# Corner and MLP sums on GpSimd, a norm pass in place, VectorE's and TensorE's order in the slots, image 1's convolutions in two parts, and a reordered ramp

## The reference

```
x_ln = layernorm(x) * g + b
q    = x_ln @ wq + bq                                # 1024 rows
o    = gelu(depthwise_conv7x7(q, stride 2) + dw_b)   # 16 x 16 positions
off  = tanh(o @ pw_w)                                # 2 numbers per position
samp = bilinear samples of x at (reference point + off)   # 256 rows, 4 corners each
qh, kh, vh = (q @ mq, (samp@wv+bv) @ mk, (samp@wv+bv) @ mv)   # 8 heads of 32
att  = softmax(qh kh^T) vh                           # 1024 x 256 scores per head
z    = att @ mo + mo_b + x
y    = gelu(layernorm(z) @ mlp + mlp_b) + z
theta, phi, g = y @ w_theta, maxpool(y @ w_phi), maxpool(y @ w_g)   # biases added
out  = y + sigma * (softmax(theta phi^T) g @ w_o + b_o)
```

## Time and profile before

| | |
|---|---|
| median of 3 runs | 595.2 us (594.95 to 597.31) |
| the profiled execution, its own time | 598.47 us |
| its span, first to last instruction | 596.5 us |
| mean granted clock of TensorE | 0.90 |
| TensorE busy | 476.4 us (80% of the span) |
| VectorE busy | 311.1 us (52%) |
| ScalarE busy | 198.5 us (33%) |
| GpSimd busy | 86.5 us (15%) |

### The profile page before, as it was taken

How to read it: one execution, slowest core, us unless ns; L and a number is a source line. 1 busy time by engine, 2 the same in 40 slices (tenths; PEclk the granted TensorE clock), 3 DMA queues, 4 the chain that set the end, 5 groups by cost and what they waited for, 6 DMA issues and landing times.

```text
span 596.5 us, 9174 instructions
## 1 busy us (share of the span) xinstructions
PE 476.4 (80%) x3711; PEld 332.3 (56%) x3711; DVE 311.1 (52%) x664; ACT 198.5 (33%) x313; POOL 86.5 (15%) x120
## 2 busy tenths in 40 slices
PE   0699477887779998976899998967986896898746
PEld 0556254564447765644578665644864574666425
DVE  5635553155387443575795326665643556444242
ACT  1011100253334323651435206623263272335420
POOL 2401101052101000610001003501001041000000
PEclk9999678877798998896999997978988998899878
DMA  8596269724803970274016901363019000000001
GB/s 230 114 170 91 74 80 131 170 73 63 99 0 46 118 188 1 72 96 61 6 73 93 181 6 30 77 73 55 37 48 166 1 2 1 2 37 36 0 1 71
DMA packets 28695, 42.89 MB, mean 72 GB/s; under 512 B 5819, under 2 KB 17902, under 8 KB 28654
## 3 DMA queue, kind: packets, MB, share of 16 engines
q1 hardware_dynamic: 20894, 35.23, 34.9%
q0 software_dynamic: 3584, 4.50, 2.8%
q10 hardware_dynamic: 4176, 2.58, 1.6%
HBM read 16.16 MB, written 4.19 MB: 34 GB/s over the span
## 4 chain that ended last, share of the span: by engine, by line
PE 57%; DVE 19%; ACT 8%; DMA 8%; issue 5%; POOL 1%; SPq 1%; DVEq 0%; ACTq 0%; POOLq 0%
PE ps_d L642 8%; PE ps_d L632 5%; DMA q_st<-mx_t 5%; PE ps_v L722 5%; PE ps_d L836 4%; PE ps_d L737 4%; PE ps_t L709 4%; PE ps_v L726 4%; PE ps_s L690 4%; PE ps_d L760 4%; DVE mx L1378 4%; PE ps_d L670 2%; PE ps_d L779 2%; PE ps_d L661 2%; DMA corners<-in_L_conv_mlp_b_dram 2%
## 5 line engine op out<-in xcount | busy, mean ns | idle before, releaser
L1054 ACT ACTIVATE prob<-ps_t 128x1024 f32<-128x1024 f32 x64 | 65.4, 1021 | 111.6 <-PE ps_t L709 110.7
L1378 DVE TENSOR_REDUCE mx<-ps_s 128x4 f32<-128x1024 f32 x64 | 78.2, 1222 | 27.9 <-PE ps_s L690 26.7
L1650 POOL DMA_DIRECT2D q_st<-mx_t x64 | 34.0, 532 | 362.6 <-ACT mx_t L1046 347.9
L690 PE MATMUL ps_s<-k_st,q_st 96*128 96x256 f32 x256 | 51.3, 325 | 10.8 <-DVE mx L1378 5.6
L642 PE MATMUL ps_d<-cstack,conv_w 128*32 128x256 f32 x1024 | 59.0, 388 | 0.4 <-DMA cstack<-qpad 0.4
L709 PE MATMUL ps_t<-q_st,k_st 98*128 98x256 f32 x256 | 45.9, 306 | 9.9 <-DMA q_st<-mx_t 8.4
L690 PEld LDWEIGHTS ps_s<-k_st,q_st 96*128 96x128 f32 x256 | 37.8, 202 | 22.1 <-DVE mx L1378 8.8
L642 PEld LDWEIGHTS ps_d<-cstack,conv_w 128*32 128x32 f32 x1024 | 34.4, 111 | 25.4 <-issue 6.0
L632 PE MATMUL ps_d<-wq,xln 128*128 128x256 f32 x128 | 33.8, 425 | 15.0 <-DVE xln L1270 15.0
L709 PEld LDWEIGHTS ps_t<-q_st,k_st 98*128 98x128 f32 x256 | 38.6, 208 | 11.7 <-DMA q_st<-mx_t 9.0
L722 PE MATMUL ps_v<-prob,vh 128*32 128x256 f32 x512 | 42.0, 455 | 0.0
(11 more groups left out here) (161 smaller groups left out, 723.8 us busy)
## 6 DMA issues: line engine op xcount, KB each, us to landing
q_st<-q_parts SPq DMA_DIRECT2D x48, 256.0 KB, 8.5
cstack<-qpad SPq DMA_DIRECT2D x24, 180.5 KB, 5.3
xa<-in_x_dram SPq DMA_DIRECT2D x8, 512.0 KB, 12.6
z_all<-in_x_dram SPq DMA_DIRECT2D x4, 1024.0 KB, 14.2
out_dram<-z_all SPq DMA_DIRECT2D x8, 512.0 KB, 2.6
k_st<-cstack SPq DMA_DIRECT2D x12, 256.0 KB, 6.2
cstack<-att SPq DMA_DIRECT2D x8, 180.5 KB, 7.0
q_st<-mx_t POOLq DMA_DIRECT2D x64, 4.0 KB, 2.5
```

The source lines that it names most:

```text
L690: ins = pe.matmul(ps_s[:, h, :], q_st[0:96, hg * HQ + h, c0 + half * P:c0 + (half + 1) * P], k_st[0:96, b % 2, h, hg, :], start=True, stop ...
L1054: drain(act.activation(prob[:, u % 2, 2 * pr:2 * pr + 2].rearrange("p h m s -> p (h m) s"), ps_t[:], ACT.Exp), t_ring, "t", b, u, pr)
L1378: drain(dve.tensor_reduce(mx[:, u % 2, half, :], ps_s[:], AX.X, ALU.max), s_ring, "s", b, u, half)
L1650: pool.dma_start(q_st[96 + part:97 + part, hg * HQ:(hg + 1) * HQ, c0:c0 + S_].bitcast(F32), mx_t[32 * part:32 * part + HQ, u % 2, :].bitca ...
```

## The change

Seven things are changed together.

1. **Corner sums on GpSimd.** For images 1 to 3 `sampled` is moved from VectorE (slot 6, or 5 for image 1) to GpSimd in slot 5, as eight products and six sums in place of two products and six fused steps. The keys of image 1 move from slot 5 to 6. Image 0's corner sums stay on VectorE, in the ramp.
2. **MLP sums on GpSimd.** `outputs` of images 0 to 2 goes to GpSimd, slots 1 and 4. `bias_rows` moves from slot 4 to 6. The tail's stay on VectorE.
3. **The norm's first pass in place**, `xa` into `xa`, as `row_scale`; the second pass is `row_shift`. The statistics move from slot 7 to slot 4 (for image 2 to slots 3 and 4), `row_scale` to slot 5 (and 6), `row_shift` stays in slot 7, whole for image 2; for image 3 a half of it is left for the next slot 0, as before for both. Image 1's normed rows lie in `z[1]`, and a part of image 0's queries in `z[0]`, which are loaded later.
4. **VectorE's order.** The maxima of scores come ahead of `residual_norm` in slot 0; `query_lo(n, 1)` comes ahead of the maxima in slot 7; the second block's maxima follow at once.
5. **TensorE's order.** The convolution's second half (`conv1`) stands behind the scores and shifted scores of slot 3; image 1's two convolutions are each cut in 6 and 10 of 16 steps, around the second half of the scores; `queries(n, 1)` leads slot 7; `q_image(n, 0)` comes before `turn_rows` in slot 0; in slot 7 a projection stands before each shifted product of the second block; `vh` of image 0 is in slot 0.
6. **The ramp.** The norm's two rows g and b are loaded first, on ScalarE's queue; the copies of folded weights are on ScalarE; the fold for the queries stands before `q_image(0, 0)`; `queries(0, 1)` goes around the offsets; `q_image(1, 0)` stands before the keys; the convolution's weights are built in two halves; image 0's planes are stacked from two queues.
7. **Positions** take 5 dependent steps in place of 7, with constants prepared on the host.

The core of the diff:

```diff
-FRONT_SLOTS_OF_1 = {"conv0": 1, "conv1": 2, "off": 3, "qh0": 4, "kh": 5, "qh1": 7}
+FRONT_SLOTS_OF_1 = {"conv0": 1, "conv1": 2, "off": 3, "qh0": 4, "kh": 6, "qh1": 7}
+FIRST_STEPS, LAST_STEPS = range(6), range(6, TAPS * TAPS)
...
@@ GpSimd @@
+            def outputs(b, cb):
+                for jp in range(2):
+                    k = dense.use("mlp", b, cb, jp)
+                    part = z[b % 2][:, cb, 2 * jp:2 * jp + 2, :]
+                    pool.wait_ge(k.drained, k.done)
+                    pool.tensor_tensor(part, part, norm_tile(b, cb)[:, 2 * jp:2 * jp + 2, :], ALU.add).then_inc(y_done.sem, 1)
+
+            def sampled(b):
+
+                pool.wait_ge(ramp_step.sem, ramp_step.at(b, 6))
+                for st in range(2):
+                    pool.wait_ge(corners_in[st].sem, corners_in[st].at(b, 2))
+                    if st == 0:
+
+                        k = dense.use("vh", b - 1)
+                        pool.wait_ge(k.filled, k.full)
+                    for n in range(4):
+                        below, right = divmod(n, 2)
+                        corner = corners[:, st, below, right * C:(right + 1) * C]
+                        weight = corner_w[:, below, right, st:st + 1]
+                        pool.tensor_scalar(corner if n else samp[:, st, :], corner, weight, None, ALU.mult
+                                           ).then_inc(weighted.sem if n else samp_step.sem, 1)
+                    for n in range(1, 4):
+                        below, right = divmod(n, 2)
+                        pool.wait_ge(weighted.sem, weighted.at(b - 1, 3 * st + n))
+                        pool.wait_ge(samp_step.sem, samp_step.at(b, 4 * st + n))
+                        pool.tensor_tensor(samp[:, st, :], samp[:, st, :], corners[:, st, below, right * C:(right + 1) * C],
+                                           ALU.add).then_inc(samp_step.sem, 1)
...
                 if in_front(b, s, "off"):
                     gather(n)
+                if s == 1 and 0 <= m < B:
+                    outputs(m, 0)
+                if s == 4 and 0 <= m < B:
+                    outputs(m, 1)
+                if s == 5 and n < B:
+                    sampled(n)
                 if s == 7 and 0 <= m < B:
                     max_row1(m)
-                if s == 4 and b < B:
+                if s == 6 and b < B:
                     bias_rows(b)
...
@@ VectorE @@
-            def row_norm(b, tiles):
-                if b and 0 in tiles:
-
-                    for hg in range(NHG):
-                        await_bank(dve, dense, "qh", b - 1, 1, hg)
+            def row_scale(b, tiles):
                 if 0 in tiles:
                     dve.wait_ge(ln1_aggr.sem, ln1_aggr.at(b, NT))
                 for t in tiles:
-                    dve.scalar_tensor_tensor(xln[:, t, :], xa[:, t, :], mv1[:, t, 0:1], lng_all[:], ALU.subtract,
+                    dve.scalar_tensor_tensor(xa[:, t, :], xa[:, t, :], mv1[:, t, 0:1], lng_all[:], ALU.subtract,
                                              ALU.mult).then_inc(ln1_scaled.sem, 1)
+
+            def row_shift(b, tiles):
                 dve.wait_ge(ln1_dev.sem, ln1_dev.at(b, 1))
+                if b >= 2 and 0 in tiles:
+
+                    for hg in range(NHG):
+                        await_bank(dve, dense, "qh", 0 if b == 2 else b - 1, 1, hg)
...
-                if s == 0 and post:
-                    residual_norm(m, 0)
...
+                if s == 0 and post:
+                    residual_norm(m, 0)
                 if in_front(b, s, "qimg0"):
-                    row_norm(n, range(NJ, NT))
-                if s == 2 and cur:
+                    if b >= 2:
+                        row_shift(n, range(NJ, NT))
+                    q_image(n, 0)
+                if s == (2 if b else 0) and cur:
                     value_rows(b)
...
-                if in_front(b, s, "kh"):
-                    sampled(n)
...
-                if s == 1 and post:
-                    outputs(m, 0)
...
-                if s == 4 and post:
-                    outputs(m, 1)
                 if in_front(b, s, "off"):
                     corner_weights(n)
+                if s == 4 and b and n + 1 < B:
+                    row_stats(n + 1)
+                if s in (3, 4) and b == 0:
+                    row_stats(n + 1, range(NJ) if s == 3 else range(NJ, NT))
+                if s == 5 and n + 1 < B:
+                    row_scale(n + 1, range(NT) if b else range(NJ))
...
@@ TensorE @@
-                for cb in range(CB):
-                    if in_front(b, s, f"conv{cb}"):
-                        conv(n, cb)
+                if in_front(b, s, "conv0"):
+                    conv(n, 0, FIRST_STEPS if b == 0 else range(TAPS * TAPS))
+                if in_front(b, s, "conv1") and b == 0:
+                    conv(n, 1, FIRST_STEPS)
...
-                if in_front(b, s, "qh1"):
-                    queries(n, 1)
-                if s == 7 and post:
                     project_g(m)
                 if cur:
                     scores(b, s, 1)
                 if unit_of(b, s, 2):
                     shifted(*unit_of(b, s, 2), 1)
-                for cb in range(CB):
-                    if in_front(b, s, f"qimg{cb}"):
-                        q_image(n, cb)
+                if in_front(b, s, "conv0") and b == 0:
+                    conv(n, 0, LAST_STEPS)
+                if in_front(b, s, "conv1"):
+                    conv(n, 1, LAST_STEPS if b == 0 else range(TAPS * TAPS))
+                if in_front(b, s, "qimg1"):
+                    q_image(n, 1)
...
                     for lh in range(2):
+                        project(b, 0, lh)
                         if post:
                             shifted1(m, lh)
-                        if cur:
-                            project(b, 0, lh)
...
             turn_weights(wq, ps_s[:, 0:2, :])
+            setup_queries()
             q_image(0, 0)
+            setup_vectors()
             q_image(0, 1)
-            setup_vectors()
-            setup_queries()
-            pe.wait_ge(setup_dve, D_QUERY)
+            setup_bias()
+            pe.wait_ge(setup_act, A_QUERY)
             queries(0, 0)
...
+            queries(0, 1, [0])
             offsets(0)
+            queries(0, 1, [1])
             setup_values()
-            queries(0, 1)
-            pe.wait_ge(setup_dve, D_ALL)
+            q_image(1, 0)
+            pe.wait_ge(setup_act, A_ALL)
             keys(0)
-            q_image(1, 0)
             q_image(1, 1)
```

291 lines of the change are left out of this document (180 added, 111 removed).

## The result

The changed kernel takes **567.2 us** (median of 4 runs, 564.5 to 571.9) where the kernel before takes 596.2 beside it: a ratio of 0.951, with a 95% interval of 0.942 to 0.960. In six more runs on another occasion it took 566.7 (ratio 0.947, 0.942 to 0.951). It is faster, as forecast, but the forecast was 542 with a range of 524 to 565: of 53 us expected, some 29 to 32 came.

A forecast was written before the change was run, and what follows sets the result against it. TensorE, its waits and its falling clock were taken as the bound. Ramp 18, image 0 11, images 1 and 2 23, image 3 1 sum to 53 us off a 596.5 us span, giving a median of 542, range 524 to 565.

The forecast's parts named there:

- Nothing is charged: GpSimd's added corner and MLP sums: no time charged, as GpSimd waits for maxima in those slots anyway.
- up to 3.3 us, off the path where I see it: Slot 5: new GpSimd work holds up the first norm pass of images 2 and 3 through the shared port pair.
- Corner sums "9.7 us": GpSimd's corner sums: 8 products at 0.75 and 6 sums at 0.62 us take 9.7 us.
- The keys' wait, 5.4: Image 0: moving corner sums off VectorE and keys to slot 6 saves 3.63 plus the keys' slow clock, 5.4 us.
- GpSimd is late: Rival: at 1.27 us a product, corner sums take 13.9 us, delaying image 0's keys; time 555 us; chance 0.17.
- I let q start at 14.7: Ramp: q starts at 14.7 us in place of 18.43, with the fold for the queries ahead; queries at 26.6.
- Some 6 us: Ramp's end: stacked keys land some 6 us after ScalarE's and VectorE's copies, so first scores come at 68 us.
- Over 73: Ramp: first scores starting after 73 us would show the prediction wrong.
- Image 0, 11 us: Image 0 gets 11 us shorter, from 3 to 16, through fewer TensorE waits and better clock, less 4 for transfers.
- transfers bound image 0: Rival: DMA transfers keep their pace, image 0 gives back its 11 us and 5 of the ramp; 558 us; chance 0.12.
- Images 1 and 2, 23 us: Images 1 and 2 together get 23 us shorter, from 12 to 30, through removed TensorE waits and better clock.
- Image 3, 1 us: Image 3 and tail: 1 us gained, from -2 to 4, as only MLP sums and slot 0's order change.

The follow-up runs named there:

- Thin corner sums: Changed kernel with 248 of 256 columns left out of GpSimd's corner products and sums, images 1 to 3, waits and order kept: 556.8 us.
- together: Changed kernel with bias sums in slot 7, image 1's corner sums, keys, z loads and image 0's value rows earlier, image 2's half norm before z's norm: 554.9 us.
- the fastest version: The run "together" plus q's first half ahead of the fold and z's norm ahead of the result rows in images 2 and 3: 542.9 us, ratio 0.910.

## Why the prediction was wrong

The median missed by 25.2 us: 19.2 in the profiled span, and 6.2 since I put the median 3.5 below the profiled execution (3.3 as in the kernel before, and the rounding), and it is 2.7 above (0.2 come off outside the span). The 6.2 is the luck of which execution was profiled: before, one that took longer than all three of the runs, after, the fastest of four. The range was cut short too: my low ends summed to 569, and I stopped it at 565; 567.2 lies between.

One row of before I misread, and it bears on the first step below. The 1.31 us that I took for each of VectorE's MLP sums beside GpSimd's is the mean of one sum that was held and one that was not. The line's view and that of the one sum, in the kernel before:

```profile
L1428 DVE TENSOR_TENSOR z_all<-z_all,zn x14: 681/692/1960, 196.2 to 547.1; 128x512 f32<-128x512 f32 x14
250.63 1.93 DVE L1428 TENSOR_TENSOR z_all<-z_all,zn 128x512 f32<-128x512 f32 x1 [1.09 <-ACT zn L1078]
```

It starts beside the third of GpSimd's four sums, before the fourth, and ends 0.56 us after the fourth, which ends at 252.00; alone it takes 0.69. So the hold-up, behind a GpSimd sum that started later, stood in the trace before.

- **"Nothing is charged" for GpSimd** is the step that failed most. Shrinking the corner sums gives back 9.9 us, the keys' wait in image 0 included. I had the two facts in hand: VectorE's sums at 1.31 beside GpSimd's, and the rule of the Trainium skill (SBUF — State Buffer, SBUF: two separate sides), that a VectorE operation with two SBUF inputs (against a GpSimd operation that reads SBUF) or in a two-port mode and a GpSimd operation hold the shared port pair one at a time. And I misread the first, as said above. I put the price at "up to 3.3 us, off the path where I see it". The norm's pass did lose some 2.8 (6.09 for 3.25); it is on the path, since theta, phi and the second block's scores stand behind it. And I had not looked at phi's sums, which its second clause covers if they run in such a mode; no run shows the mode. By the rule whichever starts first has the pair for its whole instruction. Here the sum of 0.34 has its start at 244.61, 0.40 us before the first of GpSimd's four sums, while GpSimd issued a DMA, and was held for 5.48, through all four; the measurement decides. Why it did not go first is open.
- **Corner sums "9.7 us"**: 8 products of 0.92 and 6 sums of 0.73 are 11.7 alone, 12.9 as they ran in image 1 (231.10 to 243.97). I took 0.75 a product and 0.62 a sum; the bounds 0.35 and 1.27 held, though the copy behind the 1.27 takes 0.39 in the changed kernel.
- **"The keys' wait, 5.4"** in image 0: 3.79 came in its place. GpSimd could only begin behind unit 4's row, at 129.7. The rival "GpSimd is late" described this, with the mechanism but not the place: it looked for the cost in GpSimd's own lateness and in rows of maxima, and most of it came through VectorE.
- **"I let q start at 14.7"**: 20.46. The norm was in time; the fold's last load (to 15.9) and a fold of 3.56 (1.99 in the kernel before) stood ahead. Queries at 29.56 for 26.6, and the convolution took 1.5 more. q first is worth 2.2 us in the ramp and under 1 in the time.
- **"Some 6 us" for the keys' transfer**: first scores at 74.39, 7.3 us after VectorE's copies ended at 67.12 and 8.2 after the first issue at 66.16. The rest of the 6.4 us by which the scores miss 68 was there before: the keys start at 63.29 for 58.7. "Over 73" was my sign of being wrong.
- **Image 0, 11 us**: 5.6. Thin corner sums bring 1.6, value rows out of slot 0 and the rest of "together" the remainder. How much of that is transfers and how much clock was not separated: in the run with q first 1.6 of the 2.2 were gone at the end of image 0, and a row of maxima was waited for 1.8 us longer. The rival "transfers bound image 0" is open to that extent.
- **Images 1 and 2, 23 us**: 16.9, and right but for GpSimd. With thin sums it is 24.8; the waits named went, the new one was 2.86 for 2.4, the clock 0.96 and 0.97. **Image 3, 1 us**: none.

## What to carry to other kernels

Before work goes to GpSimd because it idles, lay its new timeline beside VectorE's and look for operations there whose data are all in SBUF, the small ones too; put GpSimd's work where VectorE reads PSUM. Where a group of rows mixes an operation that met the other engine with one that did not, read the longest and not the mean. Where an instruction's start is forecast, read what stands in front of it in its own engine's order, not only when its data come. Before a run is read as clearing a suspect, check in its trace that the edit moved what it was to move. And when a wait is removed in front of a fixed order, the first candidate for the next bound is what stands second there.

## What the runs showed of the hardware

- A VectorE sum of 32x256 from SBUF to SBUF (0.34 us alone) stood 5.48 us, and a product of 128x256 (0.35) 4.44 us, beside four GpSimd sums in a row; both ended 0.16 us after the last. Beside corner sums with 0.14 us between them each 0.34 us sum of VectorE took 0.83 to 0.90 and ended 0.14 us after one of them. In the pass with two SBUF inputs eight operations lost 2.8 us altogether beside GpSimd's products and sums; GpSimd's products rose from 0.92 to 1.14 at most, its sums from 0.73 to 1.00. Statistics from SBUF (2.71 for eight, beside GpSimd's sums or not) and work from PSUM (maxima 1.22, query parts 0.75) lost nothing.
- A row of maxima of 4 KB, issued between six DMAs of 256 KB from another queue, was complete 11.0 us after its issue; the median of such rows is 2.9.
- The time of the same program goes with its mean granted clock: 564.5 us at 0.927, 565.9 to 567.0 at 0.921 to 0.924, 570.3 and 570.5 at 0.916, and 542.3 at 0.943 to 0.946 against 546.1 and 546.9 at 0.934 for the fastest version. Which of the two sets the other was not found.
